# Moving the first two batches' normalisation of attention into attention's last batch, in a two-layer gated cross-attention kernel

## The reference, cut to what matters

```
attn = softmax(Q @ K.T * scale)            # per batch and head, 512 x 1024
ctx  = attn @ V                            # 16 heads of 32 side by side -> 512 x 512
x    = x + tanh(g_xattn[1]) * (ctx @ Wo.T + bo)     # V = kv @ Wv.T + bv
x    = x + tanh(g_ffn[1]) * expert_ffn(layernorm(x))   # 8 experts, gelu, 512 -> 2048 -> 512
```

## Time and profile before

| | us |
|---|---|
| three executions | 1799.47, 1801.59, 1807.74 (median 1801.59) |
| the profiled execution | 1801.19, its span 1799.5 |
| PE busy | 1461.6 (81% of the span) |
| DVE busy | 1254.5 (70%) |
| ACT busy | 962.1 (53%) |
| POOL busy | 431.6 (24%) |

### The profile page before, as it was taken

The page is one execution under the profiler, slowest core; times in us unless marked ns, Lnnn a source line. Parts: engine busy times, 40 slices in busy tenths (PEclk is TensorE's granted clock), DMA queues, the critical chain, the costliest instruction groups (busy, mean ns, idle before and its releaser), DMA issues. The chain is left out here.

```text
span 1799.5 us, 24763 instructions
## 1 busy us (share of the span) xinstructions
PE 1461.6 (81%) x8465; PEld 800.0 (44%) x8536; DVE 1254.5 (70%) x1520; ACT 962.1 (53%) x1438; POOL 431.6 (24%) x332
## 2 busy tenths in 40 slices
PE   4887896999832676678999999999918499999996
PEld 3444443555422233332444444444403266666663
DVE  3776766555575465939999999999638686556551
ACT  4666652344333465432777777776802386665551
POOL 0121210000033001512555555565752000000000
PEclk8999998999965798786999999999958699999998
DMA  6788772000054323830243424241168196666640
GB/s 219 241 277 290 251 278 93 0 0 0 1 205 183 106 88 112 211 105 2 71 108 79 110 78 111 76 112 31 33 177 262 65 340 217 224 228 222 217 141 28
DMA packets 147476, 251.62 MB, mean 140 GB/s; under 512 B 11320, under 2 KB 61496, under 8 KB 146240
## 3 DMA queue, kind: packets, MB, share of 16 engines
q1 hardware_dynamic: 141504, 231.62, 40.9%
q0 software_dynamic: 5888, 18.91, 2.9%
HBM read 180.23 MB, written 70.07 MB: 139 GB/s over the span
## 5 line engine op out<-in xcount | busy, mean ns | idle before, releaser
L1627 ACT ACTIVATE t_e<-t_psE 128x512 f32<-128x512 f32 x512 | 304.5, 597 | 133.3 <-PE t_psE L1720 125.3
L1665 DVE TENSOR_REDUCE t_nmax<-t_psM 128x1 f32<-128x1024 f32 x256 | 301.4, 1212 | 15.4 <-PE t_psM L1701 15.4
L1586 POOL TENSOR_TENSOR t_low<-t_e 128x1024 bf16<-128x1024 f32 x128 | 248.8, 1945 | 197.1 <-ACT t_e L1627 186.2
L1731 PE MATMUL t_psO<-t_e,vst 128*96 128x512 bf16 x512 | 199.5, 390 | 2.8 <-POOL t_low L1586 2.8
L1720 PE MATMUL t_psE<-qst,kst 99*128 99x512 bf16 x512 | 195.0, 382 | 0.1
L1731 PE MATMUL t_psO<-t_low,vst 128*96 128x512 bf16 x512 | 193.1, 377 | 0.0
L1673 DVE TENSOR_TENSOR t_low<-t_e 128x1024 bf16<-128x1024 f32 x128 | 179.6, 1404 | 16.7 <-ACT t_e L1627 16.0
L1701 PE MATMUL t_psM<-kst,qst 96*128 96x512 bf16 x512 | 163.8, 403 | 28.3 <-DVE t_nmax L1665 23.1
L2213 PE MATMUL e_psG<-xeT,e_w1p 128*128 (+1 forms) x1536 | 173.3, 276 | 9.2 <-DVE e_w1p L2149 4.7
L2213 PEld LDWEIGHTS e_psG<-xeT,e_w1p 128*128 128x128 bf16 x1536 | 151.9, 99 | 30.9 <-issue 6.1
L2228 PE MATMUL e_psO<-e_w2p,e_hT 128*128 128x512 bf16 x752 | 164.9, 379 | 0.8
(11 more groups left out here) (226 smaller groups left out, 2286.3 us busy)
## 6 DMA issues: line engine op xcount, KB each, us to landing
piece<-in_L_ffn_w SPq DMA_DIRECT2D x32, 1024.0 KB, 13.8
xres<-in_L_ffn_w SPq DMA_DIRECT2D x32, 1024.0 KB, 15.1
ternary<-c_wout POOLq DMA_DIRECT2D x48, 256.0 KB, 5.6
values<-c_vst SPq DMA_DIRECT2D x32, 384.0 KB, 5.4
wT<-ternary SPq DMA_DIRECT2D x8, 1536.0 KB, 23.9
kst<-keys SPq DMA_DIRECT2D x96, 128.0 KB, 4.3
vst<-values SPq DMA_DIRECT2D x16, 768.0 KB, 9.0
mixed<-t_ost SPq DMA_DIRECT2D x64, 192.0 KB
```

The costliest lines, as they stand in the source:

```text
L1586: nc.gpsimd.tensor_tensor(low[:, slot(h, u), :, :], e32[:, slot(h, u), :, :], upper(h, u), ALU.subtract).then_inc(lo_pool, 1)
L1627: nc.scalar.activation(e32[:, slot(h, u), i, :], psE[:, i, :], ACT.Exp, scale=SC).then_inc(expd, 1)
L1665: nc.vector.tensor_reduce(nmax[:, h // G % 2, h % G, u:u + 1], banks_of(place_of_max(b, m)).rearrange("p a t -> p (a t)"), AX_X, ALU.max, ...
L1731: last = nc.tensor.matmul(psO[0:VW, h % 2, :], vst[:, g, 2 * u + i, h % G, :], part[:, i, :], start=(u == 0 and i == 0 and r == 0), stop=( ...
```

## The change

The new function parts called `prepare_output` stand inside attention, in its last batch (`LAST` = 3, `PRE` = 2):

- SP loads the row sums of batches 0 to 2 and the high and low parts of batches 0 and 1 at head 1, stores the inverses at head 10 and loads them broadcast at head 11. The output bias and the value bias are loaded in the batch before.
- DVE scales the output bias at step 0, inverts 48 rows of sums at step 36, adds parts at steps 39 and 42 and multiplies them at steps 54 and 57.
- POOL adds the bias to one tile of `xres` in each head, at `u` = 1.
- The output stage keeps only the last batch's sums and the parts of batches 2 and 3, which now have buffers of their own and are loaded at its start; POOL adds them there first.
- For room, one buffer `prebob` holds in turn the router's `disp`, the query weights, the query stage's `xT`, the prepared parts, the bias and the experts' input `xeT`. These were buffers of their own.

```diff
@@ attention_phase, SP
+                def prepare_output(h):
+
+                    if h == 1:
+                        for i in range(2):
+                            sp.wait_ge(stored[i], 16 * (LAST * NH // 2 + 1))
+                        for b in range(LAST):
+                            load_sums(sp, b, o.sums[b * NH:(b + 1) * NH, :], mixed_dram, o.sums_loaded)
+                        for b in range(PRE):
+                            load_parts(sp, b, o.pre[:, b, :, :, :], mixed_dram, o.pre_loaded[b])
+                    if h == 10:
+                        sp.wait_ge(o.rsums_ready, 1)
+                        sp.dma_start(o.rsum_dram[0:LAST].rearrange("b h s -> (b h) s"),
+                                     o.sums[:, :]).then_inc(o.rsums_stored, 16)
+                    if h == 11:
+                        sp.wait_ge(o.rsums_stored, 16)
+                        for b in range(PRE):
+                            sp.wait_ge(o.added, b + 1)
+                            load_rsums(sp, b, o.pre[:, b, 1, :, :], o.rsum_dram, o.rsum_loaded[b])
...
+                        if b == LAST:
+                            prepare_output(h)
                         if h % G == 1 and (due := group_at(b, h - 1, 0, 0)):
                             put_max(*due)
@@ attention_phase, POOL
+                        if b == LAST and u == 1:
+                            if h == 0:
+                                pool.wait_ge(o.gated, 1)
+                            nc.gpsimd.tensor_tensor(o.xres[:, h, :], o.xres[:, h, :], o.bob[:, :], ALU.add).then_inc(o.biased, 1)
@@ attention_phase, DVE (prepare_output(4 * h + u) stands at the end of each step of the last batch)
+                def prepare_output(step):
+                    pre = o.pre[:, :, :, :, :].rearrange("p b r c s -> p b r (c s)")
+                    if step == 0:
+                        dve.wait_ge(o.consts_loaded, 32)
+                        nc.vector.tensor_scalar(o.bob[:, :], o.bob[:, :], o.gates[:, 1:2], None, ALU.mult).then_inc(o.gated, 1)
+                    if step == 36:
+                        dve.wait_ge(o.sums_loaded, 16 * LAST)
+                        nc.vector.reciprocal(o.sums[:, :], o.sums[:, :]).then_inc(o.rsums_ready, 1)
+                    if step in (39, 42):
+                        b = (step - 39) // 3
+                        dve.wait_ge(o.pre_loaded[b], 32)
+                        nc.vector.tensor_tensor(pre[:, b, 0, :], pre[:, b, 0, :], pre[:, b, 1, :], ALU.add).then_inc(o.added, 1)
+                    if step in (54, 57):
+                        b = (step - 54) // 3
+                        dve.wait_ge(o.rsum_loaded[b], 16 * (P // HD))
+                        nc.vector.tensor_tensor(pre[:, b, 0, :], pre[:, b, 0, :], pre[:, b, 1, :], ALU.mult).then_inc(o.divided, 1)
@@ output_phase, SP
+                load_sums(sp, LAST, sums[:, :], mixed_dram, sums_loaded)
+                for b in range(PRE, B):
+                    load_parts(sp, b, parts[:, b - PRE, :, :, :], mixed_dram, parts_loaded[b - PRE])
+                sp.wait_ge(rsums_ready, 1)
+                sp.dma_start(o.rsum_dram[LAST], sums[:, :]).then_inc(rsums_stored, 16)
+                sp.wait_ge(rsums_stored, 16)
+                for b in range(PRE, B):
+                    sp.wait_ge(added, b - PRE + 1)
+                    load_rsums(sp, b, parts[:, b - PRE, 1, :, :], o.rsum_dram, rsum_loaded[b - PRE])
...
-                load(0)
-                sp.wait_ge(rsums_ready, 1)
-                sp.dma_start(rsum_dram.rearrange("b h s -> (b h) s"), sums[:, :]).then_inc(rsums_stored, 16)
-                load(1)
-                sp.wait_ge(rsums_stored, 16)
-                load_rsums(0)
-                load_rsums(1)
@@ output_phase, POOL
-                pool.wait_ge(bo_gated, 1)
-                for t in range(NT):
-                    nc.gpsimd.tensor_tensor(xres[:, t, :], xres[:, t, :], bob[:, :], ALU.add).then_inc(biased, 1)
+                for b in range(PRE, B):
+                    p = parts[:, b - PRE, :, :, :].rearrange("p r c s -> p r (c s)")
+                    pool.wait_ge(parts_loaded[b - PRE], 32)
+                    nc.gpsimd.tensor_tensor(p[:, 0, :], p[:, 0, :], p[:, 1, :], ALU.add).then_inc(added, 1)
@@ output_phase, DVE
-                dve.wait_ge(consts_loaded, 32)
-                nc.vector.tensor_scalar(bob[:, :], bob[:, :], gates[:, 1:2], None, ALU.mult).then_inc(bo_gated, 1)
-                dve.wait_ge(sums_loaded, 16 * B)
+                low(0)
+                low(1)
+                dve.wait_ge(sums_loaded, 16)
                 nc.vector.reciprocal(sums[:, :], sums[:, :]).then_inc(rsums_ready, 1)
-                divide(0)
-                divide(1)
                 for b in range(B):
```

More of the change, by code:

```diff
@@ L1 @@
+from collections import namedtuple
 from contextlib import ExitStack
@@ L1428, in _, with load_parts, load_rsums, load_sums @@
                     gemm(b)
-def attention_phase(nc, queries_dram, keys_dram, values_dram, mixed_dram, ident, qst, loaded, kst, vst, kv_loaded, ones_set):
+Output = namedtuple("Output", "pre sums bob bias rsum_dram gates xres bv bo consts_loaded sums_loaded pre_loaded rsum_loaded "
+                              "gated rsums_ready rsums_stored added divided biased")
+PRE = 2
+def load_parts(sp, b, target, mixed_dram, loaded):
+    for r in range(2):
+        sp.dma_start(target[:, r, :, :], mixed_dram[b, r].rearrange("(c p) s -> p c s", p=P)).then_inc(loaded, 16)
+def load_rsums(sp, b, target, rsum_dram, loaded):
+    rsum_v = rsum_dram.rearrange("b (c g) s -> b g c s", g=P // HD)
+    for g in range(P // HD):
+        sp.dma_start(target[g * HD:(g + 1) * HD, :, :],
+                     rsum_v[b:b + 1, g].to_broadcast([HD, KC, S])).then_inc(loaded, 16)
+def load_sums(sp, b, target, mixed_dram, loaded):
+    sp.dma_start(target, mixed_dram.rearrange("b r (h d) s -> b r h d s", d=HD)[b, 2, :, 0, :]).then_inc(loaded, 16)
+def attention_phase(nc, queries_dram, keys_dram, values_dram, mixed_dram, ident, qst, loaded, kst, vst, kv_loaded, ones_set, o):
     SC = float(HD) ** -0.5
@@ L1771, in output_phase @@
         sem = lambda name: c.enter_context(nc.semaphore(name))
-        parts = sb("o_parts", [P, 2, 3, KC, S], F32)
-        sums = sb("o_sums", [B * NH, S], F32)
-        bias = sb("o_bias", [P, KC], F32)
-        bob = sb("o_bob", [P, D], F32)
+        parts = sb("o_parts", [P, B - PRE, 2, KC, S], F32)
+        sums = sb("o_sums", [NH, S], F32)
         cpair = sb("o_cpair", [P, 2, 2, KC, S], BF16)
@@ L1798, in output_phase, with quotient @@
         stored = sem("o_stored")
+        def quotient(b):
+            return o.pre[:, b, 0, :, :] if b < PRE else parts[:, b - PRE, 0, :, :]
         with nc.Block() as block:
@@ L1858, in high @@
                 def high(b):
-                    act.wait_ge(divided, b + 1)
+                    if b < PRE:
+                        act.wait_ge(o.divided, b + 1)
+                    else:
+                        act.wait_ge(divided, b - PRE + 1)
                     if b >= 2:
@@ L1862, in high @@
                     for k in range(KC):
-                        nc.scalar.activation(cpair[:, b % 2, 0, k, :], parts[:, b % 2, 0, k, :], ACT.Identity,
+                        nc.scalar.activation(cpair[:, b % 2, 0, k, :], quotient(b)[:, k, :], ACT.Identity,
                                              bias=bias[:, k:k + 1]).then_inc(c_hi, 1)
@@ L1952, in _ @@
                         divide(b + 2)
+                        low(b + 2)
                     x_copy(b)
```

100 lines of the change are left out of this document (44 added, 56 removed).

## The result

| | before | after |
|---|---|---|
| median of 17 executions | 1803.7 (1796.7 to 1809.71) | 1796.43 (1792.81 to 1798.52) |
| ratio, 95% interval | | 0.9956 [0.9945, 0.9968] |
| profiled execution, its span | 1801.19, 1799.5 | 1796.95, 1795.2 |
| attention's last batch (from the copy that ends the third) | 106.15 | 134.25 |
| output stage (attention's last copy to the experts' first cast) | 131.6 | 93.9 |

The kernel is 0.44% faster. Its median lies 6 us above the forecast of 1790 and inside the range of 1779 to 1801. It is in the interval of rival B (1794 to 1801, "within 0.5%", chance 0.30) and not in that of the forecast (1782 to 1792.5, chance 0.52). One execution of the kernel before, beside the last two experiments, took 3381.61 us in a slow state and is counted nowhere.

The account below looks back on a forecast made before the run. Bounds: a serial hole with PE idle 39.87 us behind attention; in attention DVE's maxima, then the port DVE and POOL share. 1801.19 - 36.6 gained + 25.1 cost = 1789.7, about 1790; range 1779 to 1801.

Parts of the forecast that it names:

- rival B: Attention loses more (PE starves, its clock falls) or the stage gains less (late parts or inverses): about 1797, chance 0.30.
- (1): Hole between attention and output stage: splits no longer wait for the inverses, first projection comes earlier, 28.8 us gained.
- (2): Output stage: normalisations of batches 0 and 1 no longer run under POOL's additions of parts, 7.8 us gained.
- (a): Attention's last batch, step 0: scaling the bias on DVE costs 0.5 us.
- (b): Heads 0 to 8: POOL's bias addition costs 0.65 a head, 5.9 us in all, ends 3.3 and 11.3.
- (c): Head 1: 4.3 MB of loads ahead of the small DMA of maxima cost 1 us, ends 0 and 4.
- (d): Last 28 steps of attention: DVE's additions and products 9.1, POOL's bias additions 6.3, inversion 1.3, cost 16.7 us.
- the weighed rule of the Trainium skill: SBUF port: two-input DVE and SBUF-reading POOL instructions block each other fully, so moved work costs full length in last 28 steps.
- (e): Last steps of attention: PE waits may make its clock fall, cost 1 us, ends 0 and 5.
- Rival A: Attention hides more: added DVE and POOL work falls where the port is free; about 1778, chance 0.10.
- Rival C: Heads 0 to 8: each bias addition costs 3.15 a head, POOL's second half too; slower, 1812, chance 0.08.

Follow-up runs that it names:

- the last two experiments: e10 and e11, the two runs with batch 1's parts loaded at head 5, on e8 and on e1: 1779.85 and 1792.48.
- e4: Changed kernel plus a useless POOL addition of 128x2048 behind 1/sqrt of batches 0 and 1 of the output stage: 1806.66.
- e11: Changed kernel with the row of maxima issued ahead of head 1's loads and batch 1's parts loaded at head 5: 1792.48.
- e8: Changed kernel with bias additions in heads without POOL's small instructions, over the last two batches, and the row of maxima ahead of head 1's loads: 1786.88.
- e10: e8 with the loads split, batch 0's parts at head 1 and batch 1's at head 5: 1779.85.
- e5: Changed kernel with POOL's 16 bias additions moved to heads without its small instructions, 12 in the third batch, 4 in the last: 1790.62.
- e1: Changed kernel with the small DMA of row maxima issued ahead of the 4.3 MB of loads at head 1 of the last batch: 1792.54.
- e2: Changed kernel without POOL's 16 additions of the output bias to xres, a semaphore increment in their place: 1788.72.
- e3: Changed kernel with DVE's two additions and two products in attention cut to 8 of 2048 columns: 1789.74.
- e6: Changed kernel with bias additions in batches 1 and 2, parts loaded at heads 2 and 6 of the third batch, sums by POOL in eight pieces: 1780.3.

## Why the prediction was right, and where its costs were mis-sized

**(1) and (2), the gain.** 28.8 forecast and found; 7.8 forecast, 8.0 shown by e4. POOL's two additions were done 26.1 us behind attention's last copy, 25.9 by the forecast. They cleared the first normalisation, but not the step ahead of it. POOL's second addition ended at 1365.27, and DVE's last instruction before the 1/sqrt waited for it:

```profile
1363.71 1.59 DVE L1968 TENSOR_SCALAR o_veps<-o_mom 128x4 f32<-128x4 f32 x1
```

It takes 0.17 in the other three batches, so about 1.4 us was lost here.

**(a) and (b), bias work in the first nine heads.** 6.4 forecast. e11, which has them and no queue wait, is 5.8 above before: nearly right in size, wrong in place. I had given each head 0.65. Scaling the bias cost 0.35. Heads without POOL's small instructions took 7.03 as before, addition and all; each of the two heads where they meet cost 1.2 (9.79 instead of 8.55) and the head ahead of it 0.8. That is 4.3, and the other 1.5 is one fall of the clock, which (b) did not hold.

**(c), the loads at head 1, is the term that failed:** 1 forecast, ends 0 and 4. The changed kernel's nine heads are 4.9 above e11's (e4's, with the same instructions, 3.7), and with the bias additions in plain heads the loads cost 5.9 (e8 to e10) to 8.1 (e5 to e10, where the row of maxima moved too). The step that was wrong is that the loads "take 11 us and can end at 1222 to 1223.5", so that PE would hardly wait. Counted from the third batch's last copy (1199.95 before, 1204.90 now), the forecast had them go from 9 to 22 or 23.5 us. The three loads of sums were issued from 9.3 on, the four of the parts from 12.1 on, and these landed at 19.8, 23.9, 25.3 and 29.2: 17.2 us for 4.2 MB, where 390 GB/s would give 10.8. The middle of the burst ran near that rate (378 GB/s in 1223 to 1230), the stretches 1217 to 1220 (212) and 1231 to 1235 (75) did not. The row itself hardly left late: it was issued 17.65 us behind that copy, against 17.2 in e1, where it stands ahead of the loads, and 16.1 in the kernel before. It let PE go at 29.5, 0.24 behind the last load. (The Trainium skill's 358, in "DMA: Bandwidth & Descriptors", Specifications, is passed here too, by the 378.) The forecast's sentence that the stores' "buffers are needed only 14 us after" hid a second way to pay the same, which e8 brought out.

**(d), the last 28 steps.** 16.7 forecast, 17.3 found. Bias additions 8.0 (6.3 forecast), the four DVE instructions 7.0 (9.1), and 2.3 left for the inversion and how they interact (1.3). That the sum came out within 0.6 was luck: errors of both signs cancelled. Each of these parts is a difference of two profiles, good to 1.7 at best, and has a share of the clock in it: in the last seven heads it was at 0.50 for 13.7 us in the changed kernel, 3.4 in e2 and 6.4 in e3. That these add up to nearly their full length is what the weighed rule of the Trainium skill ("SBUF — State Buffer", Who interferes with whom) asks for; the timeline of these heads shows it as turns taken:

```profile
1320.21 3.98 DVE L1759 TENSOR_TENSOR prebob<-prebob 128x2048 f32<-128x2048 f32 x1
...
1322.00 3.31 POOL L1669 TENSOR_TENSOR xres<-xres,prebob 128x512 f32<-128x512 f32 x1
1325.28 6.77 POOL L1635 TENSOR_TENSOR t_low<-t_e 128x1024 bf16<-128x1024 f32 x2
```

A product of 2.285 takes 3.98, a bias addition of 1.26 takes 3.31. (The 4.749 by which the prediction had the trace agree is of an instruction with one tensor input, `tensor_scalar`; these rows are of instructions with two, of which the prediction's sentence speaks.) I did not foresee the gap of 4.48 at head 10: I had placed the inversion and the addition beside POOL's halves and forgotten the four small instructions on which the next maxima hang.

**(e), the clock.** 1 forecast, ends 0 and 5. The clock fell four times in the batch, for 20.5 us in all; two falls of 6.8 us go with the two waits above. They are in the lengths given for (b) to (d). Three heads give a fall a price, against the same heads of the changed kernel: with 3.4 us at the lower level they took 1.5 to 1.7 us more (11.44 instead of 9.92 in e11; 11.44 instead of 9.79 and 11.64 instead of 9.92 in e1). What the four cost together wasn't separated.

**Sum.** 28.1 of cost against 25.1, nearly all of it (c). By the profile's lengths the change gives 28.1 - 37.7 + 0.4 (experts) = -9.2, that is 1792.0 from the profiled 1801.19. The profiled execution took 4.95 more, all ahead of the last batch, and the medians put the change at -7.3. Why the phases ahead came later is open: in later profiles attention's first copy, 851.9 and 852.3 in the kernel before, lies on both sides of that (849.5 to 860.0, 855.0 in the mean of 12, by the copy's end), so 2 to 3 us may be the kernel's own, through the places of its buffers, and the rest is scatter. It wasn't tried apart.

So the phases ahead, which no term of the forecast had, carried the profiled time from 1792.0, just inside the forecast's own interval, into rival B's. In its mechanism rival B came nearest too, by its first half (PE starves and its clock falls); neither late parts nor late inverses took part beyond the 1.4 above. Rival A's 16 us of room were not there. Rival C's 3.15 a head never occurred.

## What to carry to other kernels

Work moved into a stage that "has room" should be placed by what it delays: whose small instruction or small transfer stands behind it, and who hangs on that. Put large loads into the queue in pieces that last no longer than the slack of the short transfers behind them (2.1 MB at a time cost next to nothing here, 4.3 MB at once 4 to 8 us), and spread filler for a shared port over the steps where it costs least, rather than over the batch at hand: a bias addition cost 0.3 us in the third batch's plain heads (3.5 for 12) and 1.1 in the last seven heads (8.0 for 7, with the falls of the clock that came with them). When a wait is removed and its length does not come back, remove two suspects together before dropping either: here one burst showed up first as a late row of maxima and then as a late store.

## What the runs showed of the hardware that I had not expected

- Issuing a load on SP took 0.43 us for the first of four of 1 MB and 2.31 for the last; a store behind these took 2.55 to issue (e8, at 1230.29) and its buffer was free 11.5 us after that.
- A POOL instruction of 0.22 us on 128x16 took 1.20, 3.46, 4.68 and 5.66 us, each time until 0.1 us behind the end of a DVE instruction of two inputs. It didn't get in between two halves or between a half and an addition, but it did between an addition and a half (changed kernel, 1291.3); what decides that wasn't settled. The inversion at its start let POOL's half on 128x1024 run in its usual 1.89, but not the small instruction behind it, which began 1.1 to 1.3 us before the inversion's end. Why the one and not the other wasn't settled.
- POOL held up DVE in the same way: a DVE instruction on 128x4, 0.17 us in the other batches, took 1.59 beside POOL's addition and ended 0.03 us behind it (changed kernel, 1363.71).
- PE's granted clock fell to 0.50 in or right behind every PE gap of over 4 us within attention's last batch, and behind some gaps of 2.4 to 2.5 (1247.78 in e11, 1314.34 in e6) but not behind others of the same length (1216.11 in e11, 1317.79 in e5, where it is the same wait as in e6). It came back to 1.00 after 3.4 or 6.8 us.
- In two profiles of the kernel before, the same heads of the last batch repeat to 0.02 us. In the versions whose last batch has PE waits and falls of the clock, the same instructions scatter by 1.3 to 1.7 us, and the time of attention's first copy by up to 10.5.
